# First attention's values in four column groups, and a new order of clearings and weight loads

## What is computed

```python
# x: (4, 512, 256)
q, k, v = (split_heads(xn @ W.T) for W in (Wq, Wk, Wv))       # 16 heads of 16
sim = jnp.where(causal, jnp.einsum('bhsd,bhtd->bhst', q, k) * scale, -jnp.inf)
out = jnp.einsum('bhst,bhtd->bhsd', softmax(sim), v)          # first attention
x = x + _layernorm(merge_heads(out) @ Wo.T)
# second block: rmsnorm, attention with 16 heads of 128, residual, rmsnorm, router
top_w, top_i = jax.lax.top_k(softmax(x2 @ gate_w.T), 4)
routed = sum over the four chosen experts of weight * (silu(g) * u) @ w2
x = x + _layernorm(hid + routed + shared)
```

## Time and profile before

| | us |
|---|---|
| median of 3 runs | 1279.51 |
| lowest and highest | 1278.75, 1281.93 |
| the profiled execution | 1271.58 |
| its span | 1269.8 |
| its mean granted TensorE clock | 0.985 |

### The profile page before, as it was taken

How to read it: one execution, slowest core, us unless ns; L and a number is a source line. 1 busy time by engine, 2 the same in 40 slices (tenths; PEclk the granted TensorE clock), 3 DMA queues, 4 the chain that set the end, 5 groups by cost and what they waited for, 6 DMA issues and landing times.

```text
span 1269.8 us, 24366 instructions
## 1 busy us (share of the span) xinstructions
PE 1200.0 (94%) x7612; PEld 1005.0 (79%) x7612; DVE 860.2 (68%) x2630; ACT 793.9 (63%) x1971; POOL 578.1 (46%) x845
## 2 busy tenths in 40 slices
PE   6899998989999999999999999999998889999987
PEld 5745454568989999999998999989997768999962
DVE  5666877737667766787666886677875955555535
ACT  3466777657766777677776777776776534444422
POOL 3052645444334535346542447342463356666650
PEclk9889999989999999999999999999999989999998
DMA  4477777631552011112211112111123236777766
GB/s 150 138 223 231 229 231 223 197 104 64 169 162 67 34 68 34 67 35 101 68 65 37 61 57 91 62 48 53 34 89 99 70 118 119 118 118 118 118 106 221
DMA packets 111682, 139.54 MB, mean 110 GB/s; under 512 B 11269, under 2 KB 94725, under 8 KB 111429
## 3 DMA queue, kind: packets, MB, share of 16 engines
q1 hardware_dynamic: 97108, 119.10, 30.3%
q0 software_dynamic: 14448, 18.88, 9.2%
HBM read 63.36 MB, written 61.87 MB: 99 GB/s over the span
## 4 chain that ended last, share of the span: by engine, by line
PE 67%; DVE 9%; ACT 7%; POOL 6%; DMA 4%; issue 4%; SPq 3%; POOLq 0%; ACTq 0%; DVEq 0%
PE bank L1441 45%; PE bank L1523 5%; PE bank L1827 4%; PE bank L1645 4%; PE bank L1490 3%; DMA raw_qkv<-in_qkvo 2%; DVE bank L1086 2%; POOL sum_rows L721 2%; ACT p L926 1%; PE bank L1510 1%; ACT pT L811 1%; PE bank L1517 1%; POOL xs_rows L659 1%; DVE hs L1299 1%; POOL w_hl L513 1%
## 5 line engine op out<-in xcount | busy, mean ns | idle before, releaser
L1086 DVE CUSTOM_DVE_ANT_0 bank<-bank,mask 128x512 f32<-128x512 f32 (+3 forms) x512 | 235.6, 522 | 49.5 <-PE bank L1510 36.3
L917 ACT ACTIVATE p<-bank,stat 128x512 f32<-128x512 f32 (+3 forms) x256 | 131.5, 526 | 132.3 <-DVE stat L1086 132.3
L512 POOL CAST w_hl<-raw_qkv 128x512 fp32r<-128x512 f32 x96 | 58.7, 611 | 316.0 <-DMA raw_qkv<-in_qkvo 173.1
L1441 PE MATMUL bank<-xT,w_hl 128*128 128x512 f32 x768 | 189.4, 395 | 2.4 <-POOL w_hl L513 2.4
L1441 PEld LDWEIGHTS bank<-xT,w_hl 128*128 128x128 f32 x768 | 144.1, 188 | 36.7 <-POOL w_hl L513 2.8
L721 POOL DMA_INDIRECT sum_rows<-mid,goal x79 | 122.8, 1555 | 70.9 <-DVE mid L1405 68.9
L1441 PE MATMUL bank<-pT,v 128*128 128x128 f32 (+3 forms) x768 | 137.1, 327 | 0.0
L926 ACT ACTIVATE p<-p,stat 128x512 f32<-128x512 f32 (+3 forms) x256 | 123.1, 553 | 14.7 <-DVE stat L1302 14.7
L1441 PE MATMUL bank<-qk 128*128 128x512 f32 (+3 forms) x768 | 129.4, 317 | 2.6 <-DVE pT L1286 2.6
L1441 PEld LDWEIGHTS bank<-qk 128*128 128x128 f32 x768 | 119.2, 189 | 11.3 <-DVE v L1280 2.8
L513 POOL TENSOR_TENSOR w_hl<-raw_qkv,w_hl 128x512 fp32r<-128x512 f32 x96 | 124.1, 1293 | 7.8
(11 more groups left out here) (232 smaller groups left out, 2455.4 us busy)
## 6 DMA issues: line engine op xcount, KB each, us to landing
xs_rows<-blank SPq DMA_DIRECT2D x31, 1040.0 KB, 5.0
raw_qkv<-in_qkvo SPq DMA_DIRECT2D x32, 768.0 KB, 5.3
xrow<-xs_rows SPq DMA_DIRECT2D x79, 130.0 KB, 2.5
raw_o<-in_qkvo SPq DMA_DIRECT2D x32, 256.0 KB, 3.3
sum_rows<-blank SPq DMA_DIRECT2D x3, 2176.0 KB, 9.8
stk<-xT SPq DMA_DIRECT2D x96, 64.0 KB
stk<-k_hl SPq DMA_DIRECT2D x96, 64.0 KB
yl<-sum_rows SPq DMA_DIRECT2D x24, 256.0 KB, 6.2
```

Source lines behind the costliest of these rows:

```text
L512: link(pool.tensor_copy(hi, raw))
L917: act.activation(p2[:, n % 2, POFF[qi]:POFF[qi + 1]], s2(t), ACT.Exp, scale=-1.0, bias=stat2[:, 0, n % 2, t:t + 1], accum_out=stat2[:, 1, ...
L1086: return dve.tensor_tensor_reduce(scores, scores, mask[:, TB - scores.shape[1]:], scale=-1.0, scalar=-2.0 * MASKED, op0=ALU.add, op1=ALU.m ...
L1441: ins = pe.matmul(out, a, b, start=start and i == 0, stop=stop and i == len(pairs) - 1, **kw)
```

## The change

Three things are changed.

1. In the first attention a head's four query blocks are cut in two groups, (0, 3) and (1, 2), and each group has its own 32 rows of bank 6, so four matmuls of a key block go to four column groups of the array. `weigh` and the turn of `o1` follow the new layout: two reciprocals and two products of half the size take the place of one each, and `Q_SLOT` reorders.
2. Clearings: 24 tiles of `xs_rows` as soon as `x` and the first weights are loaded, the sum buffers after the first three stacks, 4 tiles a step instead of 8, and the other 105 tiles as five DMAs of 21, each between `raw_qkv` and `raw_o` of pairs 1 to 5.
3. `sh_raw` is loaded with pair 6, and the 14 loads of `load_w1(0)` two a pair with pairs 7 to 13, each behind that pair's `raw_qkv`.

```diff
+        Q_GROUPS = ((0, 3), (1, 2))
+        Q_SLOT = (0, 1, 3, 2)
...
+        def pt1(s, a, n, queries):
 
             i, first = item(a, n)
-            return pT1[:, s % 2, i, first:first + P * n]
+            at = [first // P + q - (TPB - n) for q in queries]
+            return pT1[:, s % 2, i, :].rearrange("p (c n) -> p c n", n=P)[:, at[0]:at[-1] + 1:max(1, at[-1] - at[0]), :]
+
+        def o1_part(s, a, v, queries):
+
+            own = bank[O1_BANK][2 * DH1 * (2 * a + v):2 * DH1 * (2 * a + v + 1), :]
+            at = [Q_GROUPS[v].index(q) for q in queries]
+            return own.rearrange("p (i r n) -> p i r n", i=2, r=2)[:, at[0]:at[-1] + 1, s % 2, :]
...
+        CLEAR_FIRST, CLEAR_STEP, CLEAR_LATE = 24, 4, 5
...
             sp.wait_ge(d_blank, 2)
+            sp.wait_ge(w1_in, 16)
+            sp.wait_ge(x_in[B - 1], 16)
+            clear(xs_d, ROW, slice(0, CLEAR_FIRST))
             sp.wait_ge(stk_zero, 3)
             sp.wait_ge(ph1_lo, 4)
             for s in range(NSTK):
                 load_stack(s)
+                if s < NSUM:
+                    clear(sum_d[s], D, slice(0, T + 1))
             sp.wait_ge(ph1_lo, 4 * B)
             for s in range(N1):
                 if s >= NSTK:
                     load_stack(s)
-                prefill(s)
+                first = CLEAR_FIRST + CLEAR_STEP * s
+                clear(xs_d, ROW, slice(first, first + CLEAR_STEP))
...
             for j in range(1, N2 // 2):
                 sp.wait_ge(b_wqkv, 3 * j)
                 sp.dma_start(raw_qkv[:, :], qkvo2_d[j % (H2 // 2), :, 0:2 * WQKV2]).then_inc(b_rawqkv, 16)
+                if j <= CLEAR_LATE:
+                    first = CLEAR_FIRST + CLEAR_STEP * N1
+                    left = E * CAP // P + 1 - first
+                    clear(xs_d, ROW, slice(first + left * (j - 1) // CLEAR_LATE, first + left * j // CLEAR_LATE))
+                if j == 6:
+                    sp.dma_start(sh_raw[:, :, :], moe_d[0, :, 0:SHR, :]).then_inc(s_in, 16)
+                if j >= 7:
+                    load_w1(0, slice(2 * (j - 7), 2 * (j - 6)))
                 sp.wait_ge(b_wo, j)
                 sp.dma_start(raw_o[:, :], qkvo2_d[j % (H2 // 2), :, 2 * WQKV2:]).then_inc(b_rawo, 16)
-                if j <= NSUM:
-                    sp.dma_start(sum_d[j - 1].rearrange("(n p) d -> p n d", p=P),
-                                 blank[:, 0:D].unsqueeze(1).to_broadcast([P, T + 1, D])).then_inc(d_zero, 16)
-                if j == 4:
-                    sp.dma_start(sh_raw[:, :, :], moe_d[0, :, 0:SHR, :]).then_inc(s_in, 16)
-                    load_w1(0)
...
-                    link(dve.reciprocal(o1_rec[:, :, :].unsqueeze(3), heads[:, :, :, DH1:DH1 + 1]))
+                    link(*[dve.reciprocal(rec[:, :, v, :].unsqueeze(3), heads[:, :, v, :, DH1:DH1 + 1])
+                           for v in range(2)])
+                    for v in range(2):
+                        ins = dve.tensor_tensor(own[:, :, v, :, :], heads[:, :, v, :, 0:DH1],
+                                                rec[:, :, v, :].unsqueeze(3).to_broadcast([P, 2, 4, DH1]), ALU.mult)
+                    ins.then_inc(a1_xo, 1)
...
-                def value(r, a, n):
-
-                    kj, j = TPB - n, 2 * (r % 2) + a
-                    return pe.matmul(bank[O1_BANK][2 * DH1 * j:2 * DH1 * (j + 1), P * kj:TB], v1_pad[:, r % 2, kj, a, :],
-                                     pt1(r, a, n), start=n == TPB, stop=n == 1, skip_group_check=True)
+                def values(r, n):
+
+                    kj = TPB - n
+                    for a in range(2):
+                        for v in range(2):
+                            queries = [q for q in Q_GROUPS[v] if q >= kj]
+                            if queries:
+                                ins = pe.matmul(o1_part(r, a, v, queries), v1_pad[:, r % 2, kj, a, :],
+                                                pt1(r, a, n, queries), start=kj == 0, stop=kj == max(Q_GROUPS[v]),
+                                                skip_group_check=True)
+                    return ins
```

More of the change, by code:

```diff
@@ L366, in load_stack, with clear @@
                 sp.dma_start(f32(stk[0:P:64, slot, 0, :]), f32(stk[4:P:64, slot, 0, :])).then_inc(stk_in[slot], 16)
[L368 to L373, removed]
+            def clear(rows_d, width, some):
+                sp.dma_start(rows_d.rearrange("(n p) c -> p n c", p=P)[:, some, :],
+                             blank[:, 0:width].unsqueeze(1).to_broadcast([P, some.stop - some.start, width]))\
                   .then_inc(d_zero, 16)
             sp.wait_ge(d_blank, 2)
+            sp.wait_ge(w1_in, 16)
+            sp.wait_ge(x_in[B - 1], 16)
+            clear(xs_d, ROW, slice(0, CLEAR_FIRST))
             sp.wait_ge(stk_zero, 3)
@@ L384, in _, with load_w1 @@
                     load_stack(s)
-                prefill(s)
+                first = CLEAR_FIRST + CLEAR_STEP * s
+                clear(xs_d, ROW, slice(first, first + CLEAR_STEP))
             meet(sp)
[L388 to L393, removed]
+            def load_w1(c, pieces=slice(None)):
+                for gu, (g, k, cols, first, n) in [(gu, piece) for gu in range(2) for piece in routed_pieces(gu, c)][pieces]:
+                    out = w1_raw[c][:, gu, first:first + n]
+                    src = moe_d[g, :, k, cols]
+                    sp.dma_start(out.rearrange("p (k n) -> p k n", k=src.shape[1]), src).then_inc(w_in[c], 16)
             for j in range(1, N2 // 2):
@@ L610, in constants @@
                 whole = hot[:, :, :, :].rearrange("p t k e -> p (t k e)").bitcast(I32)
-                pool.wait_ge(d_zero, 16 * (N1 + NSUM))
+                pool.wait_ge(d_zero, 16 * (NSUM + 1 + N1 + CLEAR_LATE))
                 pool.wait_ge(m_y, 2 * B)
@@ L1139, in weigh @@
                     dve.wait_ge(a1_ot, i + 1)
-                    heads = free[:, :].rearrange("p (j h n) -> p j h n", j=TPB, h=4)
-                    link(dve.reciprocal(o1_rec[:, :, :].unsqueeze(3), heads[:, :, :, DH1:DH1 + 1]))
-                    own = o1[:, :, 4 * DH1 * (i % 4):4 * DH1 * (i % 4 + 1)].rearrange("p j (h n) -> p j h n", h=4)
-                    dve.tensor_tensor(own, heads[:, :, :, 0:DH1],
-                                      o1_rec[:, :, :].unsqueeze(3).to_broadcast([P, TPB, 4, DH1]), ALU.mult)\
-                        .then_inc(a1_xo, 1)
+                    heads = free[:, :].rearrange("p (i h v n) -> p i v h n", i=2, h=4, v=2)
+                    rec = o1_rec[:, :, :].rearrange("p (i v) h -> p i v h", i=2)
+                    link(*[dve.reciprocal(rec[:, :, v, :].unsqueeze(3), heads[:, :, v, :, DH1:DH1 + 1])
+                           for v in range(2)])
+                    own = o1[:, :, 4 * DH1 * (i % 4):4 * DH1 * (i % 4 + 1)]\
+                        .rearrange("p (i v) (h n) -> p i v h n", i=2, h=4)
+                    for v in range(2):
+                        ins = dve.tensor_tensor(own[:, :, v, :, :], heads[:, :, v, :, 0:DH1],
+                                                rec[:, :, v, :].unsqueeze(3).to_broadcast([P, 2, 4, DH1]), ALU.mult)
+                    ins.then_inc(a1_xo, 1)
                 if s + 1 < N1:
@@ L1543, in step1 @@
                     pe.wait_ge(a1_sel, 4 * (s - 1) + 1)
-                    for a in range(2):
-                        value(s - 1, a, TPB)
+                    values(s - 1, TPB)
                 if s >= 3 and s % 2 == 1:
@@ L1582, in step1 @@
                     for n in range(TPB - 1, 0, -1):
-                        for a in range(2):
-                            ins = value(s - 1, a, n)
+                        ins = values(s - 1, n)
                     ins.then_inc(a1_pv, 1)
@@ L1588, in step1 @@
                     pe.wait_ge(a1_xo, 2 * g + 2)
-                    turn(lambda j: o1[:, j, P * (g % 2):P * (g % 2 + 1)], a1_xt, free)
+                    turn(lambda j: o1[:, Q_SLOT[j], P * (g % 2):P * (g % 2 + 1)], a1_xt, free)
                 if b >= 0 and k == 2:
```

1 line of the change is left out of this document (removed).

## The result

The changed kernel takes 1260.79 us (median of four runs, 1255.6 to 1261.62) against 1279.13 for the kernel before on the same chip: ratio 0.9841, 95% interval 0.9819 to 0.9863, so 18.3 us off (17.5 to 23.2 by the interval) where 23.3 were forecast (1256.2). A second series gave 1258.82 against 1277.54, ratio 0.9855 (0.9823 to 0.9886).

The account below looks back on a forecast made before the run. It took PE to bound the second attention, and PE with ACT and DVE the first. Values 20.2, clearings 0.7 and weight loads 2.4 make 23.3 us off 1279.5: 1256.2 us, range 1250 to 1262.

Parts of the forecast that it names:

- C and G: First attention, a step's value parts: C is key block 0, gain 0.43 us; G key blocks 1 to 3, gain 0.53.
- Rivals 1 and 2: First: PE's queue limits small matmuls, 54 ns a record, 1262.8 us, chance 0.17. Second: within 0.3%, C near 0.99 us, 0.11.
- Rival 3: PE alone bounds the first attention: 34 + 3.1 = 37 us off, 1242 us; chance 0.05.
- The steps: First attention, passes of step1 on PE, from one turn of `least` to the next; the values' gain summed to 20.2 us.
- Even steps: Short even steps: C's gain lost in PE's wait for ACT's copies into `stk`; 0.47 us each, 4.7 for ten.
- Steps 14, 22 and 30: Counted among the short even steps at 0.47 us each, C's gain lost in the wait for `stk`.
- Odd steps: Short odd steps 3, 7, 15, 23: DVE's chain read with 0.64 us of slack; gain 0.75 us each, 3.0 in all.
- weigh's split: DVE in odd steps: two reciprocals and two half-size products cost between nothing and 0.3 us more; 0.1 taken.
- The tail's 1.2: Last two rounds of the first attention, where POOL's select hides C: gain 1.2 us.
- Rival 4: Clock at 1.2 GHz through the first attention: steps 8.4 us instead of 6.24, +67 us, 1344 us; chance 0.07.
- Part 2: Clearings in the first attention, 4 tiles a step: PE's waits for stacks go, 0.7 us; first stacks delayed at no cost.
- Part 3: Second attention, weight loads two a pair from pair 7: PE's wait at 379.24 us goes, 2.4 us gained.

Follow-up runs that it names:

- e5: The changed kernel with three transposes of the identity, read by nobody, in PE's wait at the end of steps 16 and 24; 1256.10 us, ratio 0.9829.
- e7: The changed kernel with the two products of weigh made twice on DVE; 1258.0 us (one run).
- e2: The kernel before with only the new order of clearings and weight loads, the values as before; 1272.46 us, ratio 0.9959.
- e1: The kernel before with only the values in four column groups and the new weigh; 1280.29 us against 1277.54, ratio 1.0013.
- e11: The changed kernel with the loads of sh_raw and load_w1(0) behind raw_o of pair 4 again; 1257.76 us, ratio 0.9849.
- e12: e11 with the three sum buffers also cleared behind raw_o of pairs 1 to 3 again; 1266.3 us (one run).
- e8: The kernel before, unchanged, profiled once more; span 1279.7 us.
- e6: e5 with transposes of the identity also in PE's waits around the border of the two attentions; 1252.07 us, ratio 0.9810.
- e9: e6 with more transposes at the start of the first attention and weigh's two reciprocals joined into one; 1250.76 us, ratio 0.9790.
- e10: The changed kernel with 6 tiles cleared a step instead of 4, and fewer later; 1263.0 us (one run).

## Why the prediction was right, and where not

The forecast of 1256.2 us lies 4.6 us under the result, inside its range; the gain of 23.3 us was sized 5 us above the measured one and just outside its interval (17.5 to 23.2). The mechanism holds with all three parts together, but that the sum came so close is in part luck: the steps gave more than was written, the falls of the clock took 3.0 us of it back, and the tail gave nothing. The 18.4 us of the steps and the 2.4 of the wait for `w_hl` make 20.8. What came between that and the 18.3 measured the profiles don't decide, since two of them differ by 9.9 us for one and the same kernel.

**C and G.** Gains of 0.42 and 0.64 us by the rows against 0.43 and 0.53. Four groups of 32 columns run side by side and independently; the middle between lockstep and independent was a needless hedge, and the lower end is excluded. Rivals 1 and 2 fall with it: G's 20 records pass in 0.78 us, 39 ns each. Rival 3 falls by the steps: 34 us would have come if PE alone were the bound, and 21.4 came where the clock held. The Trainium skill's page TensorE: Matmul & The Clock Gate, section "Wait — 56ns, not 53.3ns?", has some 62 ns a matmul with hardware decode off; by it 20 records would take 1.24 us, an estimate from the page's figure. The trace's 0.78 us does not agree with it; whether hardware decode is on here no run shows. The same section has a floor of some 25 ns for the smallest matmuls; no row here comes down to it.

**The steps.** 19.7 us were forecast for the 31 steps (20.2 less 1.2 for the tail plus 0.7 for stacks), and 21.4 is what they gain where the clock doesn't fall (193.23 to 171.85 in e5). Even steps were sized low (0.47; 0.66): by the rows the exponentials start 0.09 us sooner behind the turn, and ACT's copy of o_sum starts 0.12 us ahead of the end of their record and not at it. Steps 14, 22 and 30 were sized much too low. There PE waits for ACT's copy into `stk`, and the prediction held C's gain for lost in that wait; but what it waits for began a step or more earlier and comes sooner too. In step 14 the wait ends 3.49 us behind the turn before and 2.92 now, and behind it another 0.55 us are gained. In e7, where step 13 is 0.53 us longer, that wait is 0.58 us and not 1.09. Odd steps were sized high (0.75; 0.54): DVE's chain had less slack than the 0.64 us that was read, and e7 shows that it bounds them. weigh's split costs 0.09 us (0.1 forecast). The tail's 1.2 did not come: from the last turn of `least` to the last G it is 6.66 us before and 6.69 now, since PE waits for POOL's selects (1.9 us in two waits, before 0.95 in one), and to the turn of `o` 10.38 and 10.36.

**Rival 4, in small.** The prediction let the clock stay up because "single waits of 1.6 us did not before"; that was the weakest step. With thinner work on PE a wait of 0.57 us, and 0.20 behind it, was enough. It was put down as a fall through the whole stage, at +67 us and a chance of 0.07; what came was 3.4 us twice, 3.0 us in all. A case between nothing and everything was missing.

**Part 2.** Its own worth was sized right (0.7; e2's steps show 1.1), and the cover of the first stacks held: nothing waits for them in the change. But it was costed as an edit beside the others. e1 shows that it carries part 1: without parts 2 and 3, part 1 gives 0, and its own 17.3 us of waits are all for stacks, which part 2 is about. The text had the numbers at hand, 3.30 against 1.74 us for three loads, and seven loads and a clearing a step; summed for the kernel *before* (3.30 and 1.74 for six loads, 0.58 for the seventh, 0.4 for the clearing) they give 6.0 us, measured 6.17, next to the mean step of 6.24. For the new kernel 4.9 us was written, and 5.06 and more is measured: three loads take 2.16 us behind a clearing, where 1.8 was announced.

**Part 3.** Right sum, but the cause was half told: PE's wait is gone from the change and from e2, and with the sum clearings of part 2 in their new place it is gone without part 3 too (e11). It takes loads and sum clearings together to bring it back (e12). On PE's path the end of this wait brought its 2.4 us, but the profile compared with lacked 3.0 us of PE's wait for stalled DVE, and a fall of the clock at 267 us took 1.7; so the second attention looked 1.8 us longer (679.0 to 680.8 us from its first wait for qk to the last turn of weights). Against e8 it is 6.2 us shorter; 1.9 of that is the wait, and most of the rest two stretches of half clock that e8 has and the change's profile lacks (3.4 us from 375 us on, 6.8 from 952).

**The sum.** The profiled execution of before was taken for typical, 0.6% under the median. It was a special one, as e8 shows. From 293 to 930 us it keeps step with e8 within 1.5 us; the border of the two attentions is 3.0 us longer in it (18.13 against 15.15 us from the last turn of `least` to the first work on `w_hl`), and the stretch behind 930 us, with both stalls, is some 13 us shorter. A second profile of before would have told.

## What to carry to other kernels

Before costing a faster engine, add up the issue cycle of every queue that feeds the same step, with the durations that its issues have behind a large transfer, and set it beside the shortest run of steps and not beside the mean: a queue at 6.2 us under a step of 6.24 took the whole of a gain of 21 us here. When work on PE gets thinner, look for half clock behind each remaining wait, and try a few idle transposes right in it: three of them kept a step 1.5 us shorter here, though what that is worth over the whole kernel has to be measured again. And ask which edit of a bundle makes room for which; the one that is worth nothing alone may be the one to keep.

The best kernel of this study is the change with PE's waits filled (e6, 1252.07 us, ratio 0.981, and e9 beside it), some 6 us under the change by the spans.

## What the runs showed of the hardware

- Four column groups of 32 for a float32 matmul pass 256 columns each in 0.57 us from the first record to the next work, and 384 in 0.78; two groups took 0.99 us for 512 columns each and 1.42 for 768.
- A clearing costs SP nothing itself (0.39 us), but the next issues: three loads take 3.2 us behind 1040 KB (e1), 2.66 behind 780 (e10), 2.16 behind 520 (the change; means of 25 to 27 steps). Where SP waits for a slot between the clearing and the loads, as in e2 (31.3 us in 23 waits from 71 to 230 us, against 11.9 in 10), the same three take 1.80 us behind 520 KB. So the backlog in the queue slows the issue; which of the two, SP's issuing or the queue's draining, bounds the cycle these runs don't separate.
- The clock falls from 2.4 to 1.2 GHz for 3.4 us or several times that, also behind a wait of under 0.6 us, and at the same places in two profiles of the change and in e11 (151, 199, 267 us); but at other places in two profiles of the kernel before (264 us; 283 and 375 us). PE waits 3.0 us (2.4 to 3.5) behind DVE's stall between 928 and 956 us in 13 profiles; behind it the clock fell in seven of them and held in six.
- DVE stood idle for some 3 us (2.3 to 3.7) at one fixed place and DVE and ACT for 3.7 to 5.1 us at another of the program with nothing that the profile shows to release them, while POOL went on. No instruction fetch is recorded then. POOL issues indirect DMAs (`DMA_INDIRECT xs_rows<-xrow,idx`) during both, but it does so at the first place in the first profile of before as well (942 to 952 us), which has no stall. The cause stays open; no experiment here was made on it.
